# Softmax reciprocals of the first attention: from fp32 spreading matmuls to a 21st block of the DMA transposes and fp16 matmuls of 32 rows

## The reference, cut to what matters

```python
q, k, v = einsum('bsx,xAnh->Abnsh', input, w)
a = q k^T * h**-0.5 + relative_causal(q emb^T)       # per batch and head, 512 x 512
a = softmax(where(mask, a, -1e9), axis=-1)           # causal
o = einsum('bnqk,bnkh->bqnh', a, v)
x = layernorm(x + o @ out_kernel + out_bias)
```

## Time and profile before

| | us |
|---|---|
| median of 3 runs | 1677.52 (1674.55 to 1745.03) |
| the profiled execution | 1676.82 |
| its span, first to last instruction | 1675.1 |
| first attention, from its first DVE instruction to its last | 36.4 to 799.2 |

### The profile page before, as it was taken

How to read it: one execution, slowest core, us unless ns; L and a number is a source line. 1 busy time by engine, 2 the same in 40 slices (tenths; PEclk the granted TensorE clock), 3 DMA queues, 4 the chain that set the end, 5 groups by cost and what they waited for, 6 DMA issues and landing times. The chain is left out here.

```text
span 1675.1 us, 38178 instructions
## 1 busy us (share of the span) xinstructions
PE 1421.9 (85%) x12519; PEld 834.2 (50%) x12519; DVE 1262.4 (75%) x2722; ACT 971.0 (58%) x1921; POOL 879.9 (53%) x1203
## 2 busy tenths in 40 slices
PE   4899989898998999897589887489899899898736
PEld 3566666666666666665356555123333333332216
DVE  3788888887888888886688888377787787777534
ACT  2677767676776767675244443156666666665431
POOL 2877778777787777775445555211221221222524
PEclk9899999999999999999699999599999999999977
DMA  5645545454454545544000000411011011010001
GB/s 160 123 113 127 123 98 125 97 122 110 110 125 105 114 111 118 116 110 94 0 2 0 0 0 0 146 48 35 27 39 36 26 39 36 26 40 28 13 12 27
DMA packets 372881, 116.47 MB, mean 70 GB/s; under 512 B 341675, under 2 KB 369312, under 8 KB 372704
## 3 DMA queue, kind: packets, MB, share of 16 engines
q1 hardware_dynamic: 369472, 111.36, 27.9%
q10 hardware_dynamic: 1824, 3.15, 0.6%
q0 software_dynamic: 1536, 1.34, 0.3%
HBM read 20.36 MB, written 12.89 MB: 20 GB/s over the span
## 5 line engine op out<-in xcount | busy, mean ns | idle before, releaser
L541 ACT ACTIVATE prob<-score_ps,nmax 128x512 f32<-128x512 f32 (+3 forms) x512 | 264.9, 526 | 209.0 <-DVE nmax L594 209.0
L1563 DVE TENSOR_REDUCE a_nm<-a_s 128x1 f16<-128x512 f32 x512 | 324.8, 687 | 55.5 <-PE a_s L1335 53.6
L1489 ACT ACTIVATE a_pt<-a_st 128x1024 f32<-128x1024 f32 x256 | 260.4, 1021 | 131.4 <-PE a_st L1353 116.3
L130 POOL TENSOR_TENSOR gate<-mhalf 128x1 f32<-128x1 f32 (+1 forms) x284 | 124.2, 437 | 259.3 <-ACT k L566 137.6
L1335 PE MATMUL a_s<-a_kop,a_qop 128*128 128x512 f16 x512 | 199.6, 391 | 64.2 <-DVE a_nm L1563 47.4
L606 DVE SCALAR_TENSOR_TENSOR p<-prob,p 128x1280 f16<-128x1280 f32 x128 | 204.6, 1598 | 49.8 <-ACT p L550 49.8
L594 DVE TENSOR_REDUCE nmax<-score_ps 128x1 f32<-128x512 f32 (+3 forms) x512 | 213.0, 475 | 3.4 <-PE score_ps L455 3.3
L452 PE MATMUL score_ps<-k_h,q_h 128*128 128x512 f16 (+3 forms) x512 | 158.2, 309 | 22.4 <-ACT prob L541 14.2
L550 ACT ACTIVATE p<-prob 128x1280 f16<-128x1280 f32 x128 | 163.8, 1279 | 6.5
L888 ACT ACTIVATE hid<-fps,b_cols 128x512 f32<-128x512 f32 x130 | 86.3, 687 | 127.2 <-PE fps L848 127.2
L694 POOL TENSOR_TENSOR q_l<-q,q_h 128x512 f16<-128x512 f32 x130 | 152.9, 1176 | 10.8
(11 more groups left out here) (331 smaller groups left out, 3433.5 us busy)
## 6 DMA issues: line engine op xcount, KB each, us to landing
a_qop<-q_parts SPq DMA_DIRECT2D x32, 128.0 KB
a_kop<-k_parts SPq DMA_DIRECT2D x128, 24.0 KB
x_tok<-in_L_attn_input_dram SPq DMA_DIRECT2D x4, 512.0 KB, 12.3
pt<-p SPq DMA_TRANSPOSE x128, 4.1
e_w<-in_L_ffn_w_dram SPq DMA_DIRECT2D x1, 2048.0 KB, 8.3
q_parts<-a_q_h SPq DMA_DIRECT2D x16, 128.0 KB
k_parts<-a_k_h SPq DMA_DIRECT2D x16, 128.0 KB
out_dram<-a_res SPq DMA_DIRECT2D x8, 256.0 KB
```

What stands on the lines that cost most here:

```text
L541: ins = nc.scalar.activation(prob[h][:, P_OFF[c]:P_OFF[c] + w], score_ps[u][:, col:col + w], ACT.Exp, bias=nmax[h][:, c:c + 1], accum_out= ...
L1489: nc.scalar.activation(pt[kc % 2][r][:, :, :], st_ps[r][:, :, :], ACT.Exp, scale=1.0 / SC).then_inc(exp_done[r], 1)
L1563: nc.vector.tensor_reduce(nm[g % 2][:, c, hh:hh + 1], s_ps[c % 2][:, :], AX.X, ALU.max, negate=True).then_inc(max_done[c % 2], 1)
```

## The change

In `low(h, n, k)`, behind its wait for the high part, DVE now computes the reciprocal, multiplies it by 1024 into fp16 (the high part of the reciprocal) and subtracts to get its low part, before the large instruction. The two parts of the four reciprocals go as 8 columns into a 21st block of `p16`; two waits on the new semaphore `r_steps` order these three small instructions. `reciprocals` and its semaphore are gone. The DMA transpose carries 21 blocks. In `weighted_values` the matmuls that spread the reciprocals stand behind the wait for the transposes, take 32 rows of the 21st transposed block as the moving operand and a constant 0/1 matrix `chosen` in fp16 as the stationary one. DVE sets the 21st blocks to zero and writes `chosen` at the start of the phase, and PE waits for that (`rows_set`). `batch_sum` divides by 1024 twice.

```diff
--- before.py
+++ after.py
@@ -298,13 +298,14 @@
         v_h = [sb(f"v_h{k}", [P, QC, P], F16) for k in range(2)]
         v_l = [sb(f"v_l{k}", [P, QC, P], F16) for k in range(2)]
         prob = [sb(f"prob{h}", [P, PW], F32) for h in range(2)]
-        p16 = [[sb(f"p16_{h}{k}", [P, 2, PW], F16) for k in range(2)] for h in range(2)]
-        pt = [[sb(f"pt{h}{k}", [P, 2 * BLOCKS, P], F16) for k in range(2)] for h in range(2)]
+        p16 = [[sb(f"p16_{h}{k}", [P, 2 * PW + P], F16) for k in range(2)] for h in range(2)]
+        pt = [[sb(f"pt{h}{k}", [P, 2 * BLOCKS + 1, P], F16) for k in range(2)] for h in range(2)]
+        chosen = sb("chosen_rows", [32, QC, 64], F16)
         r_sb = sb("r_sb", [P, S], F32)
         o32 = sb("o32", [P, S], F32)
         nmax = [sb(f"nmax{h}", [P, QC], F32) for h in range(2)]
         sums = [sb(f"sums{h}", [P, QC], F32) for h in range(2)]
-        rsum = [sb(f"rsum{k}", [P, QC, 2], F32) for k in range(2)]
+        rsum = [sb(f"rsum{h}", [P, QC], F32) for h in range(2)]
         y = sb("ln_y", [P, QC, D], F32)
         st = sb("ln_st", [P, QC, 6], F32)
         mv = sb("ln_mv", [P, QC, 2], F32)
@@ -319,7 +320,7 @@
         k_mm, k_out, k_split = sem("k_mm"), sem("k_out"), pair("k_split")
         v_mm, v_hi, v_lo = sem("v_mm"), sem("v_hi"), sem("v_lo")
         s_mm, max_done, exp_done = pair("s_mm"), pair("max_done"), pair("exp_done")
-        p_hi, p_lo, r_done = pair("p_hi"), pair("p_lo"), pair("r_done")
+        p_hi, p_lo, r_steps, rows_set = pair("p_hi"), pair("p_lo"), sem("r_steps"), sem("rows_set")
         turned = [pair(f"turned{h}") for h in range(2)]
         pv_mm, r_out, o_done, out_mm, y_done = sem("pv_mm"), sem("r_out"), sem("o_done"), sem("out_mm"), sem("y_done")
         pool_steps, turn_open = sem("ra_pool"), sem("turn_open")
@@ -401,7 +402,7 @@
                 if h == 0 and later(n, 2):
                     sp.wait_ge(pv_mm, n - 1)
                     sp.sem_inc(turn_open, 1)
-                sp.dma_start_transpose(pt[h][k][:, :, :], p16[h][k][:, :, :].rearrange("p a b -> p (a b)")).then_inc(turned[h][k], 16)
+                sp.dma_start_transpose(pt[h][k][:, :, :], p16[h][k][:, :]).then_inc(turned[h][k], 16)
 
             def body(n, t, b, p, k):
                 if later(n, 1):
@@ -458,16 +459,15 @@
             def weighted_values(n, t, k):
 
 
-                pe.wait_ge(r_done[1], n + 1)
                 if later(n, 1):
                     pe.wait_ge(o_done, n)
-                for c in range(QC):
-                    for h in range(2):
-                        nc.tensor.matmul(r_ps[64 * h:64 * h + 64, c * P:(c + 1) * P], rsum[k][:, c, h:h + 1].to_broadcast([P, 64]),
-                                         m.ident[:, :], start=True, stop=True)
                 pe.wait_ge(v_lo, n + 1)
                 for h in range(2):
                     pe.wait_ge(turned[h][k], 16 * (t + 1))
+                for c in range(QC):
+                    for h in range(2):
+                        nc.tensor.matmul(r_ps[64 * h:64 * h + 64, c * P:(c + 1) * P], chosen[:, c, :],
+                                         pt[h][k][0:32, 2 * BLOCKS, :], start=True, stop=True)
                 for i, (j, c, blocks) in enumerate(PIECES):
                     step = blocks[-1] - blocks[0] if len(blocks) > 1 else 1
                     for term, (low, v) in enumerate([(0, v_h), (0, v_l), (1, v_h)]):
@@ -494,6 +494,7 @@
                 mm.then_inc(out_mm, 1)
 
             def first_front():
+                pe.wait_ge(rows_set, 1)
                 project_k(0, 0)
                 project_q(0, 0, 0)
                 pe.wait_ge(q_out[0], 1)
@@ -547,7 +548,7 @@
                 act.wait_ge(exp_done[h], count(n, 2))
                 if later(n, 2):
                     act.wait_ge(turned[h][k], 16 * t)
-                nc.scalar.activation(p16[h][k][:, 0, :], prob[h][:, :], ACT.Copy, scale=P_SCALE).then_inc(p_hi[h], 1)
+                nc.scalar.activation(p16[h][k][:, 0:PW], prob[h][:, :], ACT.Copy, scale=P_SCALE).then_inc(p_hi[h], 1)
 
             def r_copy(n):
                 act.wait_ge(pv_mm, n + 1)
@@ -595,15 +596,17 @@
                                                       AX.X, ALU.max, negate=True)
                     ins.then_inc(max_done[h], 1)
 
-            def reciprocals(h, n, k):
-                dve.wait_ge(exp_done[h], count(n, 2))
-                if later(n, 2):
-                    dve.wait_ge(pv_mm, n - 1)
-                nc.vector.reciprocal(rsum[k][:, :, h], sums[h][:, :]).then_inc(r_done[h], 1)
-
             def low(h, n, k):
+
                 dve.wait_ge(p_hi[h], n + 1)
-                nc.vector.scalar_tensor_tensor(p16[h][k][:, 1, :], prob[h][:, :], P_SCALE, p16[h][k][:, 0, :],
+                into = p16[h][k][:, 2 * PW:2 * PW + 2 * QC].rearrange("p (c i) -> p c i", i=2)
+                step = 4 * n + 2 * h
+                nc.vector.reciprocal(rsum[h][:, :], sums[h][:, :]).then_inc(r_steps, 1)
+                dve.wait_ge(r_steps, step + 1)
+                nc.vector.tensor_scalar(into[:, :, 0], rsum[h][:, :], P_SCALE, None, ALU.mult).then_inc(r_steps, 1)
+                dve.wait_ge(r_steps, step + 2)
+                nc.vector.scalar_tensor_tensor(into[:, :, 1], rsum[h][:, :], P_SCALE, into[:, :, 0], ALU.mult, ALU.subtract)
+                nc.vector.scalar_tensor_tensor(p16[h][k][:, PW:2 * PW], prob[h][:, :], P_SCALE, p16[h][k][:, 0:PW],
                                                ALU.mult, ALU.subtract).then_inc(p_lo[h], 1)
 
             def q_evac(h, n, pw):
@@ -631,7 +634,7 @@
                 dve.wait_ge(out_mm, PAIRS * (b + 1))
                 dve.wait_ge(bias_in, b + 1)
                 dve.wait_ge(ln_dve, b + 1)
-                nc.vector.scalar_tensor_tensor(y[:, :, :].rearrange("p c d -> p (c d)"), out_ps[:, :], O_SCALE / P_SCALE,
+                nc.vector.scalar_tensor_tensor(y[:, :, :].rearrange("p c d -> p (c d)"), out_ps[:, :], O_SCALE / (P_SCALE * P_SCALE),
                                                m_flat(m.x)[:, ds(b * S, S)], ALU.mult, ALU.add).then_inc(y_done, 1)
 
             def batch_stats(b):
@@ -650,7 +653,6 @@
                 if at(p, 2) and not at(b, 0):
                     batch_sum(b - 1)
                 if later(n, 1):
-                    reciprocals(1, n - 1, 1 - k)
                     low(1, n - 1, 1 - k)
                 q_evac(0, n + 1, pw)
                 if behind:
@@ -658,7 +660,6 @@
                 low(0, n, k)
                 if later(n, 2):
                     normalise(n - 2)
-                reciprocals(0, n, k)
                 maxima(1, n)
                 q_evac(1, n + 1, pw)
                 v_low(n, k)
@@ -668,13 +669,19 @@
                     batch_norm(b - 1)
 
             def first_front():
+                for h in range(2):
+                    for k in range(2):
+                        nc.vector.memset(p16[h][k][:, 2 * PW:2 * PW + P], 0.0)
+                for c in range(QC):
+                    one = lambda r: m.ident[0:32, r:r + 1].to_broadcast([32, 64])
+                    last = nc.vector.tensor_tensor(chosen[:, c, :], one(2 * c), one(2 * c + 1), ALU.add)
+                last.then_inc(rows_set, 1)
                 vector_gate(nc, m).then_inc(ln_dve, 1)
                 q_evac(0, 0, 0)
                 q_evac(1, 0, 0)
 
             def last():
                 n = B * PAIRS
-                reciprocals(1, n - 1, 1)
                 low(1, n - 1, 1)
                 normalise(n - 2)
                 normalise(n - 1)
```

## The result

The changed kernel takes 1713.56 us (median of 4 runs, 1711.84 to 1716.92); the kernel before, run beside it on the same chip, 1676.16 (4 runs). One of these four took 1745.03 us, in a slower state of the chip, and the ratio leaves it out. The ratio is 1.0229, with a 95% interval of 1.0204 to 1.0254: slower, by 37.4 us. In the profiled execution (1714.89 us) the span grew from 1675.1 to 1712.8, by 37.7 us.

The account below looks back on a forecast made before the run. The prediction took a gapless loop through DVE and ACT, 11.02 us per body, as the bound. Bodies 24.0 + 4.1 + 4.9 = 33.0 us, with start and end 34.5, on 1676.8 gave 1711 us, range 1692 to 1728.

Parts of the forecast that it names:

- PE's and the DMA's part in the loop: First attention: fp16 for fp32 matmuls and a 21st transposed block; worth nothing, PE 1.87 us early, transpose 5.4 us spare.
- `low(1)`: DVE's low part of head 1: three small instructions add 0.39 us, covered by DVE's idle 0.96 us.
- POOL's gate behind `k_copy`: Held by the later low(1): about 0.48 us long rather than 0.19, moving the k subtraction's end from 204.88 to 205.17.
- plain body: The 50 of 64 bodies without batch_sum or statistics: each grows by 0.48 us (lower end 0.28), to about 11.5 us.
- body p = 2: The 7 bodies with batch_sum: POOL's subtraction shifts by the full 0.39, so each grows by 0.58 us (lower end 0.38).
- body p = 7: The 7 bodies with statistics: DVE enters low(0) without idling, both additions exposed, each grows by 0.70 us.
- start: Once, at the phase's start: PE waits for four memsets and four small additions, about 1.0 us.
- end, from the last norm: Once, at the phase's end: last low(1) and spreading matmuls exposed, 0.39 + 0.2 against about the fp32 ones, 0.5 us.
- (A): Rival at low(0): POOL's subtraction holds only two-input instructions, so the multiply isn't held; 1700 us, chance 0.30.
- (B): Rival: POOL's gate and affine_select go before low(0)'s large instruction; 1750 us, or 1725 in a third of bodies; chance 0.12.
- (C): Rival: not slower, PE is nearer the loop and its saving outweighs DVE's 0.48; 1638 or 1673 us, chance 0.06.
- (D): Rival: the waits between the small instructions are free, as the Trainium skill says; 1677 us, chance 0.04.

Follow-up runs that it names:

- the repeated run: The changed kernel itself, measured again on the chip of three follow-up runs, against the kernel before there: 1711.97 us, ratio 1.0212.
- PE's part alone: Changed kernel without its DVE part: 21st block of ones and moved fp16 matmuls in, DVE's reciprocals as before; against the kernel before 1664.64 us, ratio 1.0003.
- head 1 alone: Changed kernel with head 0's three small instructions left out; against the kernel before +6.1 us, ratio 1.0040.
- head 0 early: Changed kernel with head 0's three small instructions moved ahead of low(0)'s wait for the high part; 1713.13 us, ratio 1.0224 against the kernel before.
- two reciprocals: Changed kernel with the multiply replaced by a second reciprocal writing fp16, and a plain two-tensor subtraction; 1688.50 us, ratio 1.0076 against the kernel before.
- head 0 alone: Changed kernel with head 1's three small instructions left out; against the kernel before +13.8 us, ratio 1.0088.
- in the gaps: Changed kernel with reciprocals in DVE's idle times and one subtraction for both heads ahead of low(1); 1672.72 us, ratio 0.9979 against the kernel before.
- both changed kernels of short splits: POOL's four splits cut to 8 of 512 columns from the fourth pair: changed kernel 1664.18 us; with head 0's small instructions moved early 1640.29 us.
- kernel before with short splits: Kernel before with POOL's four splits cut to 8 of 512 columns from the fourth pair on; 1631.04 us, ratio 0.9802 against the kernel before.

## Why the prediction was right

1711 us was forecast, from 34.5 us added to 1676.8; the profiled execution added 37.7 to its span. By the prediction's own steps:

| step | forecast, added us | measured, added us |
|---|---|---|
| PE's and the DMA's part in the loop | 0 | 0 (body 11.02, alone) |
| `low(1)` | +0.39 | +0.40 (210.53 - 210.04 - 0.09) |
| POOL's gate behind `k_copy` | 0.48 long | 0.50 |
| plain body | +0.48 | +0.52 |
| body p = 2 | +0.58 | +0.64 (11.50 to 12.14) |
| body p = 7 | +0.70 | +0.58 |
| all bodies, to the last norm | 33.0 | 35.0 |
| start | 1.0 | 1.2 (first `maxima` 44.08 to 45.25; in the repeated run 44.75) |
| end, from the last norm | 0.5 | 2.7 (838.14 - 818.61 against 799.24 - 782.44) |
| after the phase | 0 | -1.2 |

*The mechanism* was right: the loop through DVE and ACT, the latency of dependent small instructions, `low(1)` acting through POOL's gate, and a multiply that is held as the two-input ones are. That last choice set it apart from (A), which fails on the multiply of 0.46 us. The size of the plain body is 0.04 short: forecast, the dependent steps were 0.20 and the large instruction counted from 0.80 us after the reciprocal's start (204.54 to 205.34); it starts 0.79 after (213.21 to 214.00), and then lasts 1.49 us, where 1.46 was assumed from an instruction that follows one without a wait. That is 0.03 of it.

*Body p = 7* had the wrong mechanism and nearly the right number, which is luck. The sum had both of DVE's additions exposed. In fact the norm of that batch waits for POOL in both kernels. POOL, then DVE, of the changed kernel, and then of the kernel before:

```profile
233.72 1.04 POOL L137 TENSOR_TENSOR ln_rstd<-ln_ve,mhalf 128x4 f32<-128x4 f32 x1
234.80 1.12 DVE L123 TENSOR_SCALAR x_tok<-ln_y,ln_mv,ln_rstd 128x128 f32 x4 [1.21 <-POOL ln_rstd L137]
```

```profile
223.96 1.04 POOL L137 TENSOR_TENSOR ln_rstd<-ln_ve,mhalf 128x4 f32<-128x4 f32 x1
225.04 1.11 DVE L123 TENSOR_SCALAR x_tok<-ln_y,ln_mv,ln_rstd 128x128 f32 x4 [2.33 <-POOL ln_rstd L137]
```

DVE's additions come out of its wait, and POOL's own chain sets the length: from its gate behind `k_copy` to the end of `ln_rstd` it takes 234.76 - 223.10 = 11.66 us, before 225.00 - 213.92 = 11.08, which is the 0.58.

*The end* was the term that was mis-sized: 0.5 against 2.7 us. The step said that the last `low(1)` and the spreading matmuls are exposed "against about the fp32 ones now hidden", and put PE's clock at nothing. `low(1)` took 0.43 of it. From its end to the start of the weighted products it is 826.61 - 821.62 = 4.99 us, before 789.44 - 785.02 = 4.42: the spreading matmuls are 0.57, where 0.2 was put. The other 1.7 us is the clock. The weighted products run at 0.50 throughout and take 3.42 us instead of 2.59, and the last product 2.07 instead of 1.16. The kernel with PE's part alone has the first part of that too (3.31 us), and not the second. Why the clock came back when it did stays open: with the same matmuls in the same place, the last product ran at 0.50 in both profiled runs of the changed kernel, with head 1 alone, with head 0 early and with two reciprocals, and took 1.16 us with PE's part alone, with head 0 alone, in the gaps, and in both changed kernels of short splits. The weighted products took 3.42 us in the kernel before with short splits as well.

*(B)* didn't decide, by 0.02 us: at 214.00 the large instruction was first, at 214.02 the gate was held. The prediction put the margin at zero, so that it fell this way in the plain bodies is in part luck, and no run shows what the other order would cost in one of them. Where POOL was first, in p = 7, it got only the affine_select in, and what was held was a small subtraction that ends when that ends. The Trainium skill (SBUF — State Buffer, Who interferes with whom) has it that issue order decides who blocks; the pairs above whose order can be seen agree, either way round (DVE's 208.25 before POOL's 208.36, POOL's 211.34 before DVE's 211.43). At 225.71, and at 209.74 with head 0 alone, both start at the same time in the trace, and no order can be read. The same section counts a one-input `tensor_scalar` among what can enter a two-port mode and so take the shared pair; the 0.46 and 1.09 us of the multiplies agree, and the reciprocals of 0.15 to 0.18 us are not held.

*(C)* is out: with PE's part alone the ratio is 1.0003 [0.9993, 1.0013]; PE was 1.87 us early, and taking 1.09 - 0.41 = 0.68 us from it bought nothing. *(D)* is out: even with the lock away the three instructions cost 0.43 us per body. The Trainium skill (VectorE: DVE Perf Modes, The DRAIN you can't avoid) lets a semaphore between chained instructions cost nothing extra; for these of 128x4 the runs show 0.20 to 0.21 us from start to start with one and 0.07 to 0.09 without, so the measurement decides here.

*The size of the difference* came out at 2.3%, just beyond what a measurement of this kernel can tell; in the repeated run it is 2.1% [1.95, 2.28], on the line. The chance had been put at 0.59 for the other side of it. The forecast lay on the line too, and the 2.0 us missed in the bodies and 2.2 at the end moved the result over it, less the 1.2 us by which the rest of the kernel was shorter, for which no run shows a cause.

## What to carry to other kernels

A saving on an engine that is early buys nothing, however many matmuls it removes, while a few tiny instructions on the engine that closes the loop are paid in full: 64 times 0.5 us here. Where DVE and POOL share work, ask of each small instruction two things, which wait stands before it and whether it is of a kind that the other engine can hold, and then place it: instructions that aren't held go into idle time, those that are go where the other engine is quiet. When one cause of a delay is taken away and nothing moves, look for a second one over the same stretch before dropping the first.

## What the runs showed of the hardware that was not expected

- A reciprocal of 128x4 passes POOL's subtraction unhindered (0.15 to 0.18 us), a multiply by a constant of the same shape does not (1.09 us when it starts 0.09 us behind it).
- The order in the lock is stable and has memory: with head 1's instructions alone, one body p = 2 in which DVE came first turned it round for the rest of the batch. The bodies then lasted 10.96 us instead of 11.26; the kernel before has 11.02, with a reciprocal of 0.09 us in the loop that is left out there.
- Cutting POOL's splits to 8 columns took 33.8 us (2%) off the kernel before, most of it not in the plain bodies (0.20 us each) but 2.7 us per batch boundary.
- The same 8 matmuls at the end of the phase took 1.16 us at a clock of 1.00 or 2.07 at 0.50. Every kernel with the fp32 matmuls had 1.00 there, and those with the new ones had either, for a reason that no run shows.
